# TensorE reads the addresses of a one-hot adjacency build four slots at a time

## The chip, the core and the metric

One core of a Trainium2 chip runs one program. The metric is the device time of one execution in microseconds (us), lower is better. Times of single instructions are in nanoseconds (ns) where marked.

## What is computed

A graph with 3125 nodes, 256 features and 100,000 edges sorted by destination goes through a normalised two-layer graph network with edge weights and then through a two-layer graph attention network, each with a residual connection.

```python
h = jnp.maximum(_layernorm(x, axis=-1), 0.0)
# L0: twice, for (W1, b1, g1, be1) and (W2, b2, g2, be2)
agg = jax.ops.segment_sum(w[:, None] * x[src], dst, num_segments=n)
x = gelu(layer_norm((x + agg) @ W + b, g, be))
# then x @ Wp + bp, residual, layernorm, relu
# L1: twice (8 heads, then 1)
e = leaky_relu(el[src] + er[dst])
alpha = exp(e - segment_max(e)[dst]) / denom[dst]
out = segment_sum(alpha[:, :, None] * feat[src], dst)
```

The part that matters here is the segment sum of the first network. The kernel does not gather rows for it. It first builds two dense tables in DRAM, the weighted adjacency (at_d) and the one of edge counts (mt_d), and then multiplies the features by the first.

## The kernel before

**The build.** The destinations are cut into windows of 4 nodes (WIN), two windows make a pair (392 pairs), 8 pairs one stage buffer (49 of them). The edges are cut into 1568 slots (S): a slot is up to 128 edges, one per partition, that belong to one window. For a slot the stationary operand is a one-hot of the low 7 bits of each edge's source (128 x 128, bf16), and the moving operand is a one-hot over 25 source blocks x 4 nodes of the window (100 columns), once plain and three times multiplied by the three bf16 parts of the edge weight. Three matmuls with 200, 100 and 100 columns (L1411, L1413, L1414) add the slot to its window in PSUM. Which window that is depends on the data, so the matmul's PSUM address comes from a register.

**Who does what.** VectorE (L555 to L565) makes the one-hots of 16 slots (SB, one batch, 98 batches) in three instructions: L560 the stationary one, L561 the moving one, L565 the products with the weight parts. They go to a ring of 3 batches (RB); L559 waits until TensorE has finished the slots of the batch three earlier (slot_done). TensorE waits for a batch's L565 ("weighted"). ScalarE drains a pair when its last slot is done (L1245, L1246 copies PSUM to the stage buffer, L1248 clears the bank and counts window_free up). It reads its own slot limits from at_end, four words every four pairs (L1239). PSUM has 8 banks, one per pair, so a slot may start only when the pair eight earlier has been drained: TensorE waits for window_free against a limit that also comes from a register. SyncE stores a full stage buffer as two transfers of 800 KB (L1833 to at_d, L1834 to mt_d), and after the last one starts to load the tables in pieces for the first convolution (L1845).

**The table.** VectorE computes for every slot its PSUM address and its limit, TensorE transposes both into bank 4, and two copies (L506, L507) lay them out in at_tab, for each batch 16 addresses and then 4 limits (that of every fourth slot). TensorE loads these 20 words into registers at the head of each batch (L1404), then waits for the batch, and per slot does the address arithmetic in one sequencer instruction and issues three matmuls. Instructions of an engine go out in order. The instructions that load registers, wait, or compute addresses are done by the engine's sequencer, which runs ahead of the array by what the queue holds.

**Around it.** Before the loop, eight matmuls (L1395) clear the banks. After it, the first convolution (L1444) begins when its first pieces have landed.

Of the kernel before, what the change touches and what calls it, by code (L numbers as in the profile page):

```python
# [6 lines left out]
I32 = mybir.dt.int32  # L7
# [6 lines left out]
P = 128  # L14
# [28 lines left out]
SB = 16  # L43
NSL = 13
# [4 lines left out]
NPAIR = 392  # L49
# [3 lines left out]
W2 = 2 * WC  # L53
# [101 lines left out]
def program(nc, x, src, dst, ew, w1, b1, g1, be1, w2, b2, g2, be2, wp, bp,  # L155
            gw1, al1, ar1, gw2, al2, ar2, out):
    ctx = ExitStack()
    with ctx:
        def sb(name, shape, dt=F32):
            return ctx.enter_context(nc.sbuf_tensor(name, shape, dt))  # L160

        def sem(name):
            return ctx.enter_context(nc.semaphore(name))
# [28 lines left out]
        br = sb("br", [4, P], I32)  # L192
        cr = sb("cr", [4, P], I32)

        at_tab = sb("at_tab", [NSL, P // SB, SB + SB // 4], I32)
        at_end = sb("at_end", [4, P], I32)
        wts = sb("wts", [P, 4384])
        w1s, w2s, wps = (wts[:, 512 * i:512 * (i + 1)].rearrange("p (k n) -> p k n", k=2) for i in range(3))
# [46 lines left out]
        def bank(i):  # L245
            return ps[:, 512 * i:512 * (i + 1)]
# [136 lines left out]
        slot_done, window_out, window_free = (sem(n) for n in ("slot_done", "window_out", "window_free"))  # L383
# [11 lines left out]
        V = Steps(sem("vector_step"))  # L395
# [22 lines left out]
        def vector(e):  # L418
            regs = [e.alloc_register(f"vb{i}") for i in range(4)]
# [53 lines left out]
            cs, vs, m4v, pf = (small[:, 128 + 16 * i:128 + 16 * i + NSL] for i in range(4))  # L473
# [29 lines left out]
            e.wait_ge(*V.last())  # L503
            e.scalar_tensor_tensor(out=vs, in0=vs, scalar=float(W2), in1=bkf, op0=ALU.mult, op1=ALU.add).then_inc(*V.inc("slot numbers"))
            e.wait_ge(pe_prep, PREP["regs"])
            e.tensor_copy(at_tab[:, :, 0:SB], bank(4)[0:NSL, 0:P].rearrange("p (b s) -> p b s", s=SB)).then_inc(*V.inc())  # L506
            e.tensor_copy(at_tab[:, :, SB:], bank(4)[0:NSL, P + 3:2 * P:4].rearrange("p (b s) -> p b s", s=SB // 4)).then_inc(*V.inc())  # L507
            e.tensor_copy(at_end[:, :], bank(4)[0:4, 2 * P:3 * P]).then_inc(*V.inc("regs"))


# [19 lines left out]
            for n in range(0, 12, 2):  # L530
                kk, i = divmod(n, 3)
                w = min(512, S - 512 * kk)
# [22 lines left out]
            for b in range(S // SB):  # L555
                r = b % RB
# [6 lines left out]
                w = t_parts[:, s0 // SG:(s0 + SB) // SG].rearrange("p g k (o s) -> p g k o s", o=1)  # L563
# [563 lines left out]
            for s in range(NS):  # L1127
                r = s % NR
                e.wait_ge(gh_in[r], 32 * (s // NR + 1))
                if s % 4 == 0:  # L1130
                    n = min(4, NS - s)
# [222 lines left out]
        def tensor(e):  # L1354
# [11 lines left out]
            vs, pf = small[:, 144:144 + NSL], small[:, 176:176 + NSL]  # L1366
# [4 lines left out]
            for n in range(12):  # L1371
                kk, i = divmod(n, 3)
# [13 lines left out]
                for k in range(4 * kk, min(4 * kk + 4, NSL)):  # L1386
                    f = (s_lo[:, P * k:P * (k + 1)], s_code[:, P * k:P * (k + 1)], srowf[:, k, 2 * P:3 * P])[i]
# [5 lines left out]
            e.wait_ge(act_table, 6)  # L1393
            for i in range(8):
                e.matmul(bank(i), ones[0:1, :], zrow, start=True, stop=True).then_inc(window_free, 1)  # L1395
            regs = []
            for s in range(S):
                b, i = divmod(s, SB)
                if i == 0:
                    k = s // P  # L1400
                    for r in regs:
                        e.free_register(r)
                    regs = [e.alloc_register(f"pb{b}_{n}") for n in range(SB + SB // 4)]
                    e.load(regs, at_tab[k:k + 1, s % P // SB, :])  # L1404
                    e.wait_ge(*V("weighted", b))
                if i % 4 == 0:
                    e.wait_ge(window_free, e.snap(regs[SB + i // 4], donate=True, min_val=1, max_val=NPAIR + 8))
                c = e.snap(regs[i], donate=True, min_val=0, max_val=7 * 512 + W2)
                g, z = divmod(i, SG)
                lo = ohr[:, b % RB, g, :, z]  # L1410
                e.matmul(ps[:, bass.ds(c, W2)].rearrange("p (k d) -> p k d", k=2), lo, mvr[:, b % RB, g, 2:4, :, z], start=False, stop=True,  # L1411
                         skip_group_check=True)
                e.matmul(ps[:, bass.ds(c, WC)], lo, mvr[:, b % RB, g, 0, :, z], start=False, stop=True, skip_group_check=True)  # L1413
                e.matmul(ps[:, bass.ds(c, WC)], lo, mvr[:, b % RB, g, 1, :, z], start=False, stop=True,  # L1414
                         skip_group_check=True).then_inc(slot_done, 1)
# [234 lines left out]
            for s in range(NS):  # L1650
                r, so = s % NR, s % 4
                b, before = RING["slot", s]
# [355 lines left out]

        block = ctx.enter_context(nc.Block())
        block.vector(vector)  # L2010
        block.scalar(scalar)
        block.tensor(tensor)
        block.gpsimd(gpsimd)
        block.sync(sync)
# [25 lines left out]
```

## Time and profile before

| | us |
|---|---|
| median of 3 runs | 3085.93 |
| lowest, highest | 3084.87, 3090.36 |
| the profiled execution | 3084.36 |
| its span, first to last instruction | 3082.6 |
| TensorE busy | 2588.9 (84%) |
| VectorE busy | 2350.3 (76%) |
| ScalarE busy | 1274.2 (41%) |
| GpSimd busy | 1000.1 (32%) |

Busy times are over the whole span and are an average over stages with different limits. The build stage is the first sixth of the span, up to 567 us. A q behind an engine's name marks an instruction of its sequencer. PE is TensorE's matmul, PEld its weight load, DVE is VectorE, ACT is ScalarE, POOL is GpSimd, SP is SyncE. An idle time is put down to the releaser whose event came last by the records.

### The profile page before, as it was taken

Reading aid. Unit: us, or ns where it says so; the run is one execution under the profiler, and the core shown is the slowest. Engines: PE = TensorE matmul, PEld = TensorE weight load, DVE = VectorE, ACT = ScalarE, POOL = GpSimd, SP = SyncE. Lnnn points to the kernel's source line nnn. Section 1 sums busy time; section 2 is a strip of 40 time slices with the busy share of each in tenths; the row PEclk is TensorE's granted clock in tenths of the full one; section 3 lists DMA queues with packets and bytes.
Section 4 is the critical chain, followed back from the end, with each engine's and each line's share of the span. In section 5 each row is a group of like instructions: output and inputs, shape, how many; then the busy total and the mean of one; then the engine's idle time right before and its main releaser. Section 6 shows DMA issues by size and latency. Waiting matters only on the chain.

```text
span 3082.6 us, 51075 instructions
## 1 busy us (share of the span) xinstructions
PE 2588.9 (84%) x18059; PEld 1968.9 (64%) x18059; DVE 2350.3 (76%) x3097; ACT 1274.2 (41%) x3089; POOL 1000.1 (32%) x1235
## 2 busy tenths in 40 slices
PE   5677767799989999989599999787777777757999
PEld 3666666454545555479588888565555556646888
DVE  7999999689633444488899999987777777666886
ACT  7777777202000111200255555465555554204443
POOL 3000000011110222303177777677777772011000
PEclk8888888899999999999799999899999999758999
DMA  4434344633447777334288888688877882432553
GB/s 142 167 155 172 159 163 162 239 113 120 127 138 251 254 265 258 119 105 126 73 233 228 233 226 229 167 233 217 217 217 217 217 217 92 139 88 70 167 164 103
DMA packets 311100, 538.18 MB, mean 175 GB/s; under 512 B 108482, under 2 KB 213460, under 8 KB 310596
## 3 DMA queue, kind: packets, MB, share of 16 engines
q1 hardware_dynamic: 241700, 309.63, 30.6%
q0 software_dynamic: 69152, 225.28, 25.7%
q8 instruction: 151, 2.47, 0.3%
q14 instruction: 97, 0.79, 0.1%
HBM read 420.89 MB, written 115.11 MB: 174 GB/s over the span
## 4 chain that ended last, share of the span: by engine, by line
PE 66%; DVE 21%; issue 5%; ACT 4%; DMA 2%; POOL 1%; DVEq 0%; POOLq 0%; SPq 0%; ACTq 0%
PE ps L1658 25%; PE ps L1444 15%; PE ps L1646 9%; DVE a L565 5%; PE ps L1579 5%; DVE a L560 3%; PE ps L1411 3%; PE ps L1357 2%; DVE a L561 2%; PE ps L1577 2%; DVE a L801 1%; PE ps L1413 1%; PE ps L1414 1%; PE ps L1470 1%; DVE a L833 1%
## 5 line engine op out<-in xcount | busy, mean ns | idle before, releaser
L1767 POOL DMA_INDIRECT a<-t,mid x502 | 483.2, 963 | 282.0 <-issue 143.6
L1444 PE MATMUL ps<-a 128*128 128x512 f32 x1200 | 557.4, 604 | 13.2 <-DVE a L742 13.2
L1658 PE MATMUL ps<-a,oh 128*128 128x260 f32 x2008 | 488.1, 390 | 79.0 <-issue 43.1
L1326 ACT ACTIVATE oht<-iota,mid 128x128 f32<-128x128 f32 x830 | 333.3, 402 | 441.0 <-PE ps L1658 399.1
L1658 PEld LDWEIGHTS ps<-a,oh 128*128 128x128 f32 x2008 | 366.5, 191 | 181.0 <-issue 85.1
L1411 PE MATMUL ps<-a 128*128 128x200 bf16 x1568 | 346.0, 277 | 143.5 <-DVE a L560 67.1
L1658 PE MATMUL ps<-wts,oh 128*128 128x260 f32 x1312 | 321.0, 393 | 59.3 <-ACT oh L1328 30.7
L1444 PEld LDWEIGHTS ps<-a 128*128 128x128 f32 x1200 | 219.3, 192 | 221.8 <-issue 215.3
L1137 DVE TENSOR_TENSOR a<-a,ps 128x1040 f32<-128x1040 f32 x251 | 309.6, 1234 | 55.6 <-DMA a<-t,mid 53.1
L1767 POOL DMA_INDIRECT wts<-t,mid x328 | 311.1, 949 | 111.0 <-issue 94.7
L1717 POOL TENSOR_SCALAR rstd<-mv 128x1 f32<-128x1 f32 x75 | 30.2, 403 | 955.7 <-DVE mv L452 953.5
L1413 PE MATMUL ps<-a 128*128 128x100 bf16 x1568 | 324.6, 224 | 0.0
L1414 PE MATMUL ps<-a 128*128 128x100 bf16 x1568 | 322.8, 224 | 0.0
L1658 PEld LDWEIGHTS ps<-wts,oh 128*128 128x128 f32 x1312 | 241.9, 192 | 125.7 <-ACT oh L1328 47.3
L1125 DVE TENSOR_TENSOR a<-a,ps 128x520 f32 x415 | 286.4, 690 | 7.4 <-PE ps L1658 3.0
L1646 PE MATMUL ps<-a,wts 128*128 128x257 f32 (+1 forms) x1250 | 271.5, 380 | 1.7 <-DVE wts L1083 1.7
L1411 PEld LDWEIGHTS ps<-a 128*128 128x128 bf16 x1568 | 168.3, 107 | 158.0 <-issue 157.9
L1328 ACT ACTIVATE oh<-oht 128x128 f32<-128x128 f32 x830 | 257.0, 310 | 26.2
L565 DVE TENSOR_TENSOR a<-a,mid 128x4800 bf16<-128x4800 bf16 x98 | 260.5, 2658 | 3.4
L1646 PEld LDWEIGHTS ps<-a,wts 128*128 128x128 f32 (+1 forms) x1250 | 234.4, 188 | 38.6 <-issue 1.8
L1246 ACT ACTIVATE a<-ps 128x400 f32<-128x400 f32 x392 | 193.1, 493 | 113.7 <-PE ps L1414 112.2
L1137 DVE TENSOR_TENSOR wts<-wts,ps 128x1040 f32<-128x1040 f32 x164 | 202.4, 1234 | 40.2 <-DMA wts<-t,mid 38.6
(325 smaller groups left out, 3946.8 us busy)
## 6 DMA issues: line engine op xcount, KB each, us to landing
a<-at_d SPq DMA_DIRECT2D x60, 1280.0 KB, 6.2
at_d<-a SPq DMA_DIRECT2D x49, 800.0 KB, 3.4
mt_d<-a SPq DMA_DIRECT2D x49, 800.0 KB, 5.6
a<-mt_d SPq DMA_DIRECT2D x30, 1280.0 KB, 6.1
a<-trlo_d SPq DMA_DIRECT2D x49, 512.0 KB
ot_d<-a SPq DMA_DIRECT2D x49, 320.0 KB, 6.0
a<-ot_d SPq DMA_DIRECT2D x49, 256.0 KB, 3.0
a<-t,mid POOLq DMA_INDIRECT x502, 3.8
```

The lines of the kernel that those rows point to most:

```text
L565: e.tensor_tensor(mvr[:, r, :, 0:3], bc(mvr[:, r, :, 3:4], five), bc(w, five), ALU.mult).then_inc(*V.inc(("weighted", b)))
L1125: e.tensor_tensor(d, d, pbig[RING["slot", s][0]].rearrange("p (u w) -> p u w", u=2)[:, :, 0:260], ALU.add).then_inc(head_add, 1)
L1137: e.tensor_tensor(bv, bv, col(exps_ps[:, s % 8, :], 65), ALU.mult).then_inc(head_mul, 1)
L1326: e.activation(oht[:, k, :], iota[:, :], ACT.Abs, bias=ndl[:, k, s:s + 1]).then_inc(*own.inc())
L1328: e.activation(oh[:, so, k, :], oht[:, k, :], ACT.Relu, bias=1.0, scale=-1.0).then_inc(head_oh, 1)
L1411: e.matmul(ps[:, bass.ds(c, W2)].rearrange("p (k d) -> p k d", k=2), lo, mvr[:, b % RB, g, 2:4, :, z], start=False, stop=True, skip_group_ ...
L1413: e.matmul(ps[:, bass.ds(c, WC)], lo, mvr[:, b % RB, g, 0, :, z], start=False, stop=True, skip_group_check=True)
L1414: e.matmul(ps[:, bass.ds(c, WC)], lo, mvr[:, b % RB, g, 1, :, z], start=False, stop=True, skip_group_check=True).then_inc(slot_done, 1)
L1444: m = e.matmul(acc[f].rearrange("p (x d) -> p x d", x=8), X[:, hi, P * f:P * (f + 1)], a, start=(hi == 0), stop=end, skip_group_check=True)
L1646: m = e.matmul(bank(u + j)[0:p, 0:D + 1], coef[t % R2][:, P * j:P * j + p], feat2[:, hi, :], start=(hi == 0), stop=(hi == NB - 1))
L1658: t = e.matmul(pbig[b][:, 512 * u:512 * u + 260], oh[:, so, k, :], hrows[2 * r + k][:, 260 * u:260 * (u + 1)], start=(k == 0), stop=(k == 1))
L1767: e.indirect_dma_start(out=hrows[2 * r + k], out_offset=None, in_=t2, in_offset=bass.IndirectOffsetOnAxis(ap=srci[:, k, s:s + 1], axis=0)) ...
```

## The change

at_tab becomes a plain row of 128 addresses for each 128 slots, and a new table at_free holds the limit of every eighth slot (16 for each 128 slots). TensorE loads four addresses ahead of every four slots (392 loads of 4 words), and four limits ahead of every 32 slots (49 loads of 4 words), in place of 20 words ahead of every 16 slots (98 loads). It waits for window_free once in eight slots, for the limit of the last of them, in place of once in four. The wait for the batch stays behind the loads of its first slots. VectorE still makes two copies for the tables.

```diff
--- before.py
+++ after.py
@@ -192,7 +192,8 @@
         br = sb("br", [4, P], I32)
         cr = sb("cr", [4, P], I32)
 
-        at_tab = sb("at_tab", [NSL, P // SB, SB + SB // 4], I32)
+        at_tab = sb("at_tab", [NSL, P], I32)
+        at_free = sb("at_free", [NSL, 16], I32)
         at_end = sb("at_end", [4, P], I32)
         wts = sb("wts", [P, 4384])
         w1s, w2s, wps = (wts[:, 512 * i:512 * (i + 1)].rearrange("p (k n) -> p k n", k=2) for i in range(3))
@@ -503,8 +504,8 @@
             e.wait_ge(*V.last())
             e.scalar_tensor_tensor(out=vs, in0=vs, scalar=float(W2), in1=bkf, op0=ALU.mult, op1=ALU.add).then_inc(*V.inc("slot numbers"))
             e.wait_ge(pe_prep, PREP["regs"])
-            e.tensor_copy(at_tab[:, :, 0:SB], bank(4)[0:NSL, 0:P].rearrange("p (b s) -> p b s", s=SB)).then_inc(*V.inc())
-            e.tensor_copy(at_tab[:, :, SB:], bank(4)[0:NSL, P + 3:2 * P:4].rearrange("p (b s) -> p b s", s=SB // 4)).then_inc(*V.inc())
+            e.tensor_copy(at_tab[:, :], bank(4)[0:NSL, 0:P]).then_inc(*V.inc())
+            e.tensor_copy(at_free[:, :], bank(4)[0:NSL, P + 7:2 * P:8]).then_inc(*V.inc())
             e.tensor_copy(at_end[:, :], bank(4)[0:4, 2 * P:3 * P]).then_inc(*V.inc("regs"))
 
 
@@ -1393,19 +1394,26 @@
             e.wait_ge(act_table, 6)
             for i in range(8):
                 e.matmul(bank(i), ones[0:1, :], zrow, start=True, stop=True).then_inc(window_free, 1)
-            regs = []
+            breg, freg = [], []
             for s in range(S):
                 b, i = divmod(s, SB)
+                k, w = divmod(s, P)
+                if s % 32 == 0:
+                    for r in freg:
+                        e.free_register(r)
+                    freg = [e.alloc_register(f"pf{s}_{n}") for n in range(4)]
+                    e.load(freg, at_free[k:k + 1, w // 8:w // 8 + 4])
+                if s % 4 == 0:
+                    for r in breg:
+                        e.free_register(r)
+                    breg = [e.alloc_register(f"pb{s}_{n}") for n in range(4)]
+                    e.load(breg, at_tab[k:k + 1, w:w + 4])
                 if i == 0:
-                    k = s // P
-                    for r in regs:
-                        e.free_register(r)
-                    regs = [e.alloc_register(f"pb{b}_{n}") for n in range(SB + SB // 4)]
-                    e.load(regs, at_tab[k:k + 1, s % P // SB, :])
                     e.wait_ge(*V("weighted", b))
-                if i % 4 == 0:
-                    e.wait_ge(window_free, e.snap(regs[SB + i // 4], donate=True, min_val=1, max_val=NPAIR + 8))
-                c = e.snap(regs[i], donate=True, min_val=0, max_val=7 * 512 + W2)
+                if i % 8 == 0:
+
+                    e.wait_ge(window_free, e.snap(freg[s // 8 % 4], donate=True, min_val=1, max_val=NPAIR + 8))
+                c = e.snap(breg[s % 4], donate=True, min_val=0, max_val=7 * 512 + W2)
                 g, z = divmod(i, SG)
                 lo = ohr[:, b % RB, g, :, z]
                 e.matmul(ps[:, bass.ds(c, W2)].rearrange("p (k d) -> p k d", k=2), lo, mvr[:, b % RB, g, 2:4, :, z], start=False, stop=True,
```

## Rows read from the trace of the kernel before

**Rows 1.** The page, TensorE's granted clock, 40 slices of 77 us.
```profile
PEclk8888888899999999999799999899999999758999
```

**Rows 2.** Groups by line, 60 to 570 us: shape, count, busy us, mean ns, idle before.
```profile
L1248 ACT ACTIVATE ps<-mzero 128x400 f32<-128x400 f32 x392 | 198.8, 507 | 12.4
...
L1246 ACT ACTIVATE a<-ps 128x400 f32<-128x400 f32 x392 | 193.1, 493 | 113.7 <-PE ps L1414 112.2
...
L560 DVE TENSOR_TENSOR a<-oh,a 128x2048 bf16<-128x2048 bf16 x98 | 119.6, 1221 | 29.0 <-PE ps L1414 29.0
```

**Rows 3.** The chain of waits, 60 to 580 us: start us, us, what.
```profile
84.17 1.14 DVE a L560
...
88.90 1.14 DVE a L560
...
553.12 2.67 DVE a L565
```

**Rows 4.** Single lines L560, L565, L1404: count, ns min/median/max, first to last start.
```profile
L560 DVE TENSOR_TENSOR a<-oh,a x98: 1217/1220/1227, 60.4 to 551.0; 128x2048 bf16<-128x2048 bf16 x98
...
L565 DVE TENSOR_TENSOR a<-a,mid x48: 2657/2657/2660, 62.6 to 298.5; 128x4800 bf16<-128x4800 bf16 x48
...
L1404 PEldq TENSOR_LOAD <-at_tab x48: 1357/1464/4112, 55.1 to 302.7; - x48
...
L1404 PEldq TENSOR_LOAD <-at_tab x1: 1364/1364/1364, 299.2 to 299.2; - x1
...
L1404 PEldq TENSOR_LOAD <-at_tab x1: 3626/3626/3626, 302.7 to 302.7; - x1
```

**Rows 5.** Stretches: us, busy (x count) PE PEld DVE ACT POOL, PEclk, DMA, GB/s.
```profile
300.00:301.00 1.00, 0.48 (x8) 0.33 (x7) 1.00 (x1) 0.97 (x4) 0.00 (x0) 1.00 0.00 0
...
302.00:307.00 5.00, 2.34 (x39) 2.20 (x37) 4.96 (x5) 3.65 (x8) 0.00 (x0) 1.00 0.81 328
```

**Rows 6.** Timeline of VectorE and TensorE around one load: start us, us, what, idle.
```profile
298.48 2.66 DVE L565 TENSOR_TENSOR a<-a,mid 128x4800 bf16<-128x4800 bf16 x1
...
303.45 0.25 PE L1411 MATMUL ps<-a 128*128 128x200 bf16 x1
...
303.63 0.25 PE L1411 MATMUL ps<-a 128*128 128x200 bf16 x1
...
303.76 0.21 PE L1414 MATMUL ps<-a 128*128 128x100 bf16 x1
...
306.63 0.26 PE L1411 MATMUL ps<-a 128*128 128x200 bf16 x1 [2.66 <-DVE a L565]
```

**Rows 7.** Line L1411, the sequencer's address arithmetic, once a slot; then one batch.
```profile
L1411 PEldq FUSED_REGOPS  x1568: 37/37/42, 65.3 to 565.1; - x196
...
L1411 PEldq FUSED_REGOPS  x16: 37/37/37, 306.5 to 308.5; - x16
```

**Rows 8.** Stretches around a long load.
```profile
309.60:310.20 0.60, 0.15 (x4) 0.02 (x2) 0.60 (x1) 0.57 (x2) 0.00 (x0) 1.00 0.00 0
...
313.10:316.00 2.90, 0.18 (x4) 0.03 (x1) 2.90 (x2) 1.99 (x5) 0.00 (x0) 0.99 0.87 353
...
316.00:319.30 3.30, 3.27 (x30) 3.06 (x31) 3.27 (x3) 1.70 (x4) 0.00 (x0) 0.50 0.00 0
...
320.90:324.00 3.10, 3.02 (x48) 2.96 (x48) 3.06 (x3) 3.00 (x7) 0.00 (x0) 1.00 0.65 255
```

**Rows 9.** Loads of four words on ScalarE (all, one under stores) and SyncE.
```profile
L1239 ACTq TENSOR_LOAD <-at_end x98: 305/406/907, 61.2 to 560.7; - x98
...
L1239 ACTq TENSOR_LOAD <-at_end x1: 747/747/747, 314.7 to 314.7; - x1
...
L1964 SPq TENSOR_LOAD <-cr x104: 293/298/500, 1517.1 to 2546.0; - x104
```

**Rows 10.** Timeline at the stage's end.
```profile
567.18 0.32 SPq L1833 DMA_DIRECT2D at_d<-a  x1
...
577.53 0.90 DVE L742 TENSOR_TENSOR a<-a,ident 128x128 f32<-128x128 f32 x4 [21.75 <-DMA a<-at_d]
```

## The prediction

> **What bounds the kernel now.** The change touches one loop, so I first placed it in time. The slices of the page [rows 1] are 77 us each and show TensorE's granted clock at 0.8 in the first eight and at 0.9 in most of the others; the table by line [rows 2] says what runs there: 1568 slots of three matmuls, between 62 and 567 us, VectorE building one-hots for 98 batches of 16 slots, and ScalarE draining 392 window pairs. Engine by engine: at full clock TensorE starts a slot (three matmuls) every 0.184 us (303.45 to 303.63, [rows 6]), 2.95 us a batch; ScalarE needs 0.49 + 0.51 us, 1.0 us a pair [rows 2], 4.0 us a batch of four pairs; VectorE, in the chain of waits [rows 3], goes round in 84.17 to 88.90 = 4.73 us when nothing holds it. Its L560 starts 98 times from 60.4 to 551.0 us [rows 4], which is 490.6 / 97 = 5.06 us a batch. So VectorE itself is held for 0.33 x 97 = 32 us, and L560 is the operation that waits for slots to be free (29.0 us idle behind TensorE, [rows 2]).
>
> TensorE, which has the shortest arithmetic, is therefore the engine that is late. The view of L1404 tells why [rows 4]: the register load of 20 words takes 1357 ns at best; of the 48 up to 302.7 us half take more than 1464 ns, up to 4112. The pair at 299.2 and 302.7 us took 1364 and 3626 ns. The windows over the same stretch [rows 5] show the difference: the DMA engines' share is 0.00 in 300 to 301 and 0.81 of 302 to 307, 4.0 us in all. These are the two 800 KB stores of a finished stage buffer, one pair of them for each 8 window pairs, two batches. The profile names VectorE as what ended the 2.66 us of idle at 306.63 [rows 6], but the batch that was wanted had been finished by the L565 that ran from 298.48 to 301.14 [rows 6]. By count: up to then there are 48 loads and 48 L565 [rows 4], one of each a batch, and the 48th L565 is that one. The named releaser had long been done. What ended last is the load, 302.7 + 3.63 = 306.4.
>
> How much of a load TensorE hides: it still started matmuls until 303.76, 1.0 us after the load began at 302.7. That is the queue the sequencer had filled ahead. A quiet load leaves about 0.6 us of nearly empty array (309.6 to 310.2, [rows 8]), a load under the stores 2.8 us.
>
> Sequencer time per two batches today: 16 slots issue in 306.5 to 308.5, so 0.12 to 0.13 us a slot against the array's 0.184 [rows 7]; 32 x 0.12 = 3.9, plus 1.36 + 3.63 of loads, plus about 0.2 around each, gives 9.3 us. Seen are 2 x (565.1 - 65.3) / 97.9 = 10.2 us [rows 7]. The missing 0.9 us is the clock: after 2.9 us of near idleness the next 3.3 us are granted 0.50 and hold 30 matmuls, where 3.1 us at 1.00 hold 48 [rows 8]. **Both costs hang on the one long load**, not on the matmuls.
>
> **The change part by part.** *Fewer words.* 98 loads of 20 words (1960 words) become 392 of 4 (L1404's successor) and 49 of 4 for the limits, 1764 words. What a load of 4 costs on TensorE is not in the trace. Below: 4/20 of 1357 ns, 0.27 us. Nearest rows, two other engines loading 4 words: 293 ns at best on SyncE and 305 at best on ScalarE; above: ScalarE's under the stores, 747 ns [rows 9]. I take 0.305 quiet and 0.75 under the stores, ScalarE's, because it loads in the same stretch. A load also has a seam: today the first slot of a batch comes 0.16 us after its load, which includes the batch's wait; I give 0.10 to each load and 0.1 more to each batch.
>
> *Where the loads fall.* Sequencer per two batches: 3.9 (slots) + 9 x 0.405 = 3.65 (eight address loads and one of limits) + 0.2 = 7.75 us without traffic. The stores are active about 4.0 us of it [rows 5]. Four slots in quiet take 0.49 + 0.405 = 0.90 us, under the stores 0.49 + 0.85 = 1.34 us, so 4.0 us of traffic lose 4.0 x (1 - 0.90 / 1.34) = 1.3 us. Sum 9.1 us for two batches, 4.55 a batch, against VectorE's 4.73. Were the load under the stores 1.0 us, the loss is 4.0 x (1 - 0.90 / 1.59) = 1.7 and the sum 9.5, level with VectorE's 2 x 4.73: the term is mild, since the traffic lasts 4.0 us whatever the loads do. It is also why splitting helps: before, the sequencer sat in one load while only 1.0 us of work was queued, and issued nothing; now it issues four slots between any two.
>
> *The clock.* No idle time of the array would pass about 0.6 us, the kind that the granted 1.00 survives today (309.6 to 310.2 between two stretches at 1.00, [rows 8]). So the 0.9 us per two batches goes too.
>
> *The limits.* One wait per eight slots for the eighth's pair instead of four waits a batch. The wait sits at the sequencer, with all later slots queued behind it, and ScalarE's drain must have come further by up to four slots, about one pair, of the 8 that the ring of banks allows. ScalarE needs 4.0 us a batch, plus at most 0.45 for its own load under the stores, against 4.73: it is not the bound. Taken at nothing; if ScalarE were 7 pairs late it would cost one pair, 1.0 us, per meeting.
>
> *The copies* to at_tab and at_free stay two, of 13 partitions and at most 128 words, and TensorE's first slot waits for much more than them. Nothing.
>
> **The sum.** VectorE becomes the bound. Its last L565 starts at 60.4 + 2.2 + 97 x 4.73 = 521.4 and ends at 524.1 (now 555.8, [rows 3]). TensorE then has one batch left: 0.2 + 16 x 0.12 + 3 x 0.405 + 0.4 for the last matmuls = 3.7, and ScalarE's last pair about 1 us more: the store L1833 would be issued at 529, now 567.18 [rows 10]. That is 38 us. All that follows (the first load of pieces, then the first convolution) hangs on it and moves as one; VectorE has been idle 21.75 us there [rows 10], and GpSimd has nothing in this stretch (0 instructions, [rows 5]). I take off 2 us for TensorE and VectorE being close to each other: 36. Profiled execution 3084.36 - 36 = 3048.4; the median of the runs is 1.6 above the profiled one: 3050.
>
> **The rivals.** *A: TensorE stays the bound, less so.* If loads average more than (9.46 - 4.1) / 9 - 0.10 = 0.50 us, VectorE is no longer the limit (my mean is (3.65 + 1.3) / 9 - 0.10 = 0.45, so this is near). At 9.7 us for two batches the stage ends at 68.9 + 49 x 9.7 + 3 = 547: 20 us gained, 3066. At 9.95, 3078. For it: 0.05 us of seam would do it.
>
> *B: slower.* A load on TensorE costs what it costs under the stores wherever it stands, 0.75 + 0.10, because the queue or VectorE's traffic rather than the stores slows it: 3.9 + 9 x 0.85 + 0.2 = 11.75 us for two batches, 1.55 more than now, 49 x 1.55 = 76 us: 3162. It decides from a mean load of (10.2 - 4.1) / 9 - 0.10 = 0.58 us on. Against it: the load at 299.2 ran at 1364 ns beside VectorE's L565 and a filled queue [rows 4, 6], 68 ns a word. The Trainium skill has a rule for this case, in Runtime: NRT & Kernel Launch, section "Instruction fetch mechanics": a register load costs about 200 ns a register, also in bulk. By it 4 words would be 0.8 us and the result near that of B. The trace has 68 ns a word in quiet and 180 under the stores, so the rule holds here for at most four tenths of the time.
>
> *C: the clock falls to its lower level and stays*, as the array's work is now spread thin: 30 matmuls in 3.3 us are 10 slots at 0.33 us [rows 8], and 16 of them are 5.35 us a batch, above VectorE's 4.73; 98 x 5.35 + 69 + 1 = 594, 27 us slower: 3113. Against it: at that level the array would be gapless, which is when it was granted 1.00 again at 319.3.
>
> *D: no change.* The gain is taken back, by ScalarE's limits (1.0 us for each of some 35 meetings) or behind the stage: 3080 to 3092.
>
> **How the numbers follow.** VectorE-bound, 3044 to 3054: 0.62. A, 3054 to 3078: 0.20. D: 0.07. B: 0.07. C: 0.04. A measurement of this kernel tells about 0.2%, 6 us, from no change. Faster 0.62 + 0.20 = 0.82, same 0.07, slower 0.11. Low end: VectorE's own pace allows no more than 38 us, and I add 5 for the stage's end and for what a median may differ by, 3043. High end: A's, 3078. B, C and D are left out, 0.18.
>
> **What would show it.** Right: L560 98 times from 60.4 to about 519 us with almost no idle; TensorE's idle in pieces under 1 us; the granted clock at or near 1.00 from 75 to 528; loads in clusters near 0.31 and 0.75. Wrong: a quiet load of 4 above 0.4 us; clock 0.50 in stretches; ScalarE as releaser of TensorE; the stage's end at 529 and the kernel not 36 us shorter.

## The result, and the profile after

The kernel after the change takes 3045.76 us (3044.32 to 3046.41, 4 runs) against 3085.72 us for the kernel before (3084.87 to 3090.36, 4 runs). The ratio is 0.9866, with a 95% interval of 0.9854 to 0.9879. That is 40 us less. The forecast was 3050 with 3043 to 3078 around it.

The profiled execution took 3046.41 us with a span of 3044.6. The whole gain of the span, 38.0 us, is in the build stage. The store L1833 of [rows 10] was issued at 567.18; the same store in the changed kernel is here, in the timeline at the end of the stage (start us, us, engine, line, operation):

```profile
528.73 0.49 ACT L1247 ACTIVATE a<-ps 128x400 f32<-128x400 f32 x1
529.25 0.32 SPq L1841 DMA_DIRECT2D at_d<-a  x1
```

567.18 - 529.25 = 37.9 us. What lies behind this point takes 2515.4 us before and 2515.3 us after (3082.6 - 567.2 and 3044.6 - 529.2).

The view of single lines of the changed kernel (count, ns min/median/max, first to last start) answers to [rows 4] and [rows 7]. L561 is VectorE's first instruction of a batch, L1405 the load of limits, L1410 the load of addresses, L1419 the address arithmetic, once a slot:

```profile
L561 DVE TENSOR_TENSOR a<-oh,a x98: 1215/1218/1222, 60.7 to 519.4; 128x2048 bf16<-128x2048 bf16 x98
...
L1405 PEldq TENSOR_LOAD <-at_free x49: 327/332/517, 55.3 to 518.4; - x49
L1410 PEldq TENSOR_LOAD <-at_tab x392: 327/334/1004, 55.9 to 527.0; - x196
...
L1419 PEldq FUSED_REGOPS  x1568: 37/37/42, 65.5 to 527.8; - x196
```

VectorE's round is (519.4 - 60.7) / 97 = 4.73 us, the undisturbed one of [rows 3]. The groups by line, 60 to 535 us, say the same from the other side: L561 waits for nobody (0.0, against 29.0 in [rows 2]), and ScalarE waits 67.4 us for TensorE in place of 112.2.

```profile
L561 DVE TENSOR_TENSOR a<-oh,a 128x2048 bf16<-128x2048 bf16 x98 | 119.3, 1218 | 0.0
...
L1247 ACT ACTIVATE a<-ps 128x400 f32<-128x400 f32 x392 | 194.3, 496 | 69.7 <-PE ps L1422 67.4
```

Two stretches of 50 us before and after (length, then busy and count of PE, PEld, DVE, ACT, POOL, then the granted clock, the DMA share, GB/s). Before:

```profile
120.00:170.00 50.00, 35.40 (x464) 33.26 (x463) 46.28 (x30) 37.24 (x79) 0.00 (x0) 0.86 0.41 165
```

After:

```profile
120.00:170.00 50.00, 38.41 (x523) 32.85 (x523) 49.65 (x32) 42.55 (x88) 0.00 (x0) 1.00 0.42 167
```

The granted clock is 1.00 where it was 0.86, and VectorE is busy for 49.65 of 50 us. From 75 us to the end of the stage the records of the granted clock have 33 stretches at 0.50 before, 119 us together, and one of 3.4 us after (at 285.3 us). In the table of waits (us in total, times, longest) the idle time of TensorE's weight loads on issue was in few and long pieces, and is in many and short ones. Before:

```profile
PEld ps L1411 <- issue: 157.9, 90, 3.4
```

After:

```profile
PEld ps L1419 <- issue: 146.7, 250, 1.5
```

The table of waits still names ScalarE as what ended 23.9 us of TensorE's idle time (39 times; 31.8 us before). In 31 of these 39 places (18.3 us) a load of TensorE ended later than the instruction that is named; in the other eight (5.6 us) ScalarE did end last. The matmul at 522.20 is one of the 31:

```profile
521.12 0.51 ACT L1249 ACTIVATE ps<-mzero 128x400 f32<-128x400 f32 x1
...
522.20 0.26 PE L1419 MATMUL ps<-a 128*128 128x200 bf16 x1 [0.73 <-ACT ps L1249]
```

```profile
L1410 PEldq TENSOR_LOAD <-at_tab x1: 950/950/950, 520.9 to 520.9; - x1
```

The clearing ended at 521.63. The load of the next four addresses ran from 520.94 to 521.89, under the stores, and ended last.

### The profile page after: what moved, and what is told of

It is laid out like the page before. It is cut to its first block, busy times and chain, and to the rows that moved or that the text cites. A ratio compares the mean times of both kernels' runs of the same rounds, so it can differ in the third digit from the quotient of the medians.

```text
span 3044.6 us, 51418 instructions
## 1 busy us (share of the span) xinstructions
PE 2586.2 (85%) x18059; PEld 1933.9 (64%) x18059; DVE 2346.9 (77%) x3097; ACT 1279.8 (42%) x3089; POOL 1000.1 (33%) x1235
## 4 chain that ended last, share of the span: by engine, by line
PE 62%; DVE 26%; issue 5%; ACT 4%; DMA 2%; POOL 1%; SPq 0%; DVEq 0%; POOLq 0%; ACTq 0%
PE ps L1666 26%; PE ps L1452 15%; PE ps L1654 9%; DVE a L566 8%; PE ps L1587 5%; DVE a L561 4%; DVE a L562 3%; PE ps L1358 2%; PE ps L1585 2%; DVE a L802 1%; PE ps L1478 1%; DVE a L834 1%; DVE a L601 1%; ACT oht L1327 1%; DVE a L1028 1%
## 5 line engine op out<-in xcount | busy, mean ns | idle before, releaser
L1419 PE MATMUL ps<-a 128*128 128x200 bf16 x1568 | 320.9, 256 | 108.7 <-issue 50.4
L1138 DVE TENSOR_TENSOR a<-a,ps 128x1040 f32<-128x1040 f32 x251 | 309.2, 1233 | 57.2 <-DMA a<-t,mid 54.9
L1421 PE MATMUL ps<-a 128*128 128x100 bf16 x1568 | 298.8, 208 | 0.0
L1422 PE MATMUL ps<-a 128*128 128x100 bf16 x1568 | 298.5, 208 | 0.0
L1419 PEld LDWEIGHTS ps<-a 128*128 128x128 bf16 x1568 | 152.9, 98 | 161.2 <-issue 146.7
L1138 DVE TENSOR_TENSOR wts<-wts,ps 128x1040 f32<-128x1040 f32 x164 | 202.2, 1233 | 36.1 <-DMA wts<-t,mid 34.7
L1247 ACT ACTIVATE a<-ps 128x400 f32<-128x400 f32 x392 | 194.3, 496 | 69.7 <-PE ps L1422 67.4
```

The source lines that it names most:

```text
L1138: e.tensor_tensor(bv, bv, col(exps_ps[:, s % 8, :], 65), ALU.mult).then_inc(head_mul, 1)
```

## The experiments

The stage is the place of everything here, so besides the whole time I give for each kernel the end of the stage and the pace of the slots, worked out from the first and the last start of the line with the address arithmetic: two batches take (last - first) / 97.9 x 2. That is 10.21 us before and 9.44 us after. The runs e5, e6, e7, e10 and e12 were made on chips on which all that lies behind the stage took some 180 us more, in the kernel before too (3273.87 us and 3271.61 us). The stage's pace is hardly touched by that: e12 has 10.21 us there, and e7, which by its ratio is level with the kernel before, has 10.28. The first slot comes up to 3 us later. All ratios are against the kernel before on the same chip. In the diffs `...` stands for code that is left out.

### e1: the split alone, with five words a load

```diff
-        at_tab = sb("at_tab", [NSL, P // SB, SB + SB // 4], I32)
+        at_tab = sb("at_tab", [NSL, P // 4, 5], I32)
...
-                if i == 0:
+                if i % 4 == 0:
...
-                    regs = [e.alloc_register(f"pb{b}_{n}") for n in range(SB + SB // 4)]
-                    e.load(regs, at_tab[k:k + 1, s % P // SB, :])
+                    regs = [e.alloc_register(f"pb{s}_{n}") for n in range(5)]
+                    e.load(regs, at_tab[k:k + 1, s % P // 4, :])
...
```

> One part alone: the loads are split (5 words ahead of every four slots: four addresses and their limit), the limits are waited for as before, once in four slots. Theory (the long load is what cost; the splitting is the change): a 5-word load is 0.37 to 0.40 us in quiet and about 1.1 under the stores, VectorE is the bound without idle, and the time is that of the changed kernel, 3046 to 3050 us, ratio 0.987 to 0.989. Rival 1 (the gain came from the rarer wait on window_free): no gain or little, 3080 us and more.

Measured: 3344.04 us, ratio 1.0834 (1.0816 to 1.0852). My expectation was wrong by some 295 us, and this miss taught the most. The time alone would fit rival 1, but the loads tell another cause. Twelve loads in order, in a stretch of 258 to 280 us, took 588, 1232, 1229, 1231, then 582, 3285, 1452, 1228, then 584, 1227, 1233, 1234 ns. **One load in four is fast.** The table's rows are 20 bytes apart, and every fourth row starts at a multiple of 16 bytes (counted from the start of the table, here and below). Of the 392 loads the 98 of that kind took 581 to 780 ns, all others at least 1227. The view of the line:

```profile
L1404 PEldq TENSOR_LOAD <-at_tab x392: 581/1235/3850, 55.1 to 823.9; - x196
```

### e2: the limits alone, with 18 words a load

```diff
-        at_tab = sb("at_tab", [NSL, P // SB, SB + SB // 4], I32)
+        at_tab = sb("at_tab", [NSL, P // SB, SB + SB // 8], I32)
...
-                if i % 4 == 0:
-                    e.wait_ge(window_free, e.snap(regs[SB + i // 4], ...))
+                if i % 8 == 0:
+                    e.wait_ge(window_free, e.snap(regs[SB + i // 8], ...))
```

> The other part alone: one load of 18 words ahead of every 16 slots (16 addresses, two limits), the limit waited for once in eight slots. Theory: TensorE's sequencer stays the bound, and each word less is 0.066 us in quiet and 0.18 us under the stores, so two batches save 2 x (0.066 + 0.18) = 0.5 us and the stage up to 24 us: 3062 to 3080 us, ratio 0.992 to 0.998, with loads in two clusters near 1.22 and 3.3 us and stretches at the lower clock still there. Rival 1 (the rarer wait is what gained): 3046 us.

Measured: 3253.61 us, ratio 1.0545 (1.0528 to 1.0563). Two words fewer, and 167 us more, where I had expected a gain: a second miss. Rows are 72 bytes apart now, so every second load starts 8 bytes off:

```profile
L1404 PEldq TENSOR_LOAD <-at_tab x98: 1584/3036/6778, 55.1 to 725.4; - x98
```

The 49 aligned loads took 1584 to 1781 ns, the others 4291 to 6778. Every second load is also the one that runs under the stores, as in the kernel before, so most of these long loads carry both costs. The first of them does not. It ran at 72.3 us, before the first stores:

```profile
L1404 PEldq TENSOR_LOAD <-at_tab x1: 4291/4291/4291, 72.3 to 72.3; - x1
```

```profile
71.60:76.40 4.80, 2.23 (x27) 2.00 (x24) 4.77 (x4) 2.84 (x6) 0.00 (x0) 0.86 0.01 3
```

So 4291 ns is the price of 18 words off a multiple of 16 bytes in quiet, known from this one load. These numbers and those of e1 fit one price list. A load that starts at a multiple of 16 bytes takes about 69 ns and 258 for each four words (4 words 327, 20 words 1357; 16 would be 1101), and a word left over costs almost as much as four: 581 - 327 = 254 for the fifth, (1584 - 1101) / 2 = 242 each for the seventeenth and eighteenth. A load that starts elsewhere pays for each word: (1227 - 69) / 5 = 232, (4291 - 69) / 18 = 235.

### e5: e1's loads with aligned rows

```diff
-        at_tab = sb("at_tab", [NSL, P // 4, 5], I32)
+        at_tab = sb("at_tab", [NSL, P // 4, 8], I32)
...
-                    e.load(regs, at_tab[k:k + 1, s % P // 4, :])
+                    e.load(regs, at_tab[k:k + 1, s % P // 4, 0:5])
```

> The same 392 loads of five words as in e1_split_only, but each row of the table is 8 words apart (32 bytes) in place of 5 (20 bytes), so every load starts at a multiple of 16 bytes. Theory (a load that starts at a multiple of 16 bytes reads four words at a time, some 256 ns each in quiet, and a word left over costs nearly as much; a load that starts elsewhere reads word by word at 231 ns): all loads are 581 to 590 ns in quiet, as the aligned fourth of e1's was; two batches take TensorE's sequencer 3.9 + 8 x 0.69 + 0.2 + 2.0 for the stores = 11.6 us, 3130 to 3170 us in all, against 3344 for e1. Rival (e1 was slow from five registers or from the number of loads, not from where they start): 3344 us again. The price of my forecast (0.07 us a word): 3050 us.

Measured: 3315.83 us, ratio 1.0133 (1.0113 to 1.0153), against 1.0834 for e1. The same five words in the same number of loads, only moved to multiples of 32 bytes:

```profile
L1404 PEldq TENSOR_LOAD <-at_tab x392: 576/590/1901, 57.6 to 614.3; - x196
...
L1412 PEldq FUSED_REGOPS  x1568: 37/37/42, 67.9 to 615.3; - x196
```

Two batches take 11.18 us where e1 took 15.53, and 11.6 was expected (the ratio makes some 3127 us on the first chip, just under the 3130 to 3170 forecast). So where a load starts accounts for 0.070 of e1's 0.083. The ratio is still over 1. e6 below has the same split with loads of four words and a load of limits for every 16 slots, and is at 0.9906, so the rest is the price of the fifth word.

### e7: the rarer wait alone

```diff
-                if i % 4 == 0:
-                    e.wait_ge(window_free, e.snap(regs[SB + i // 4], ...))
+                if i % 8 == 0:
+                    e.wait_ge(window_free, e.snap(regs[SB + i // 4 + 1], ...))
```

> The kernel before, loads of 20 words as they were, with only every second wait on window_free kept (for the limit of the eighth slot). Theory (the wait costs the sequencer nothing that shows): no change, 3083 to 3091 us. Rival 1 (the rarer wait gains by itself): 3070 us or less.

Measured: 3271.98 us, ratio 1.0001 (0.9991 to 1.0010). In the kernel before, the rarer wait by itself is worth nothing.

```profile
L1411 PEldq FUSED_REGOPS  x1568: 37/37/42, 65.8 to 568.9; - x196
```

### e6: the split with loads of four aligned words, limits as before

```diff
-                if s % 32 == 0:
+                if s % 16 == 0:
...
-                if i % 8 == 0:
...
+                if i % 4 == 0:
...
```

> The changed kernel with the limits as before: at_free holds every fourth slot's limit, four of them are loaded ahead of every 16 slots (98 loads in place of 49), and window_free is waited for once in four slots. So it is the split alone, with loads of four aligned words. Theory (the split is what gains; the limits give one load less per two batches): TensorE's sequencer needs 9.24 + 0.43 = 9.7 us for two batches against VectorE's 9.46, and the time is 3050 to 3062 us. Rival 1 (the rarer wait matters by itself): over 3070 us.

Measured: 3243.68 us, ratio 0.9906 (0.9887 to 0.9926), which on the first chip would be about 3057 us by my estimate. Two batches take 9.65 us, as worked out:

```profile
L1418 PEldq FUSED_REGOPS  x1568: 37/37/42, 68.5 to 540.8; - x196
```

From its first slot (68.5 us there, 65.5 in the changed kernel) the stage lasts 473.7 us against 463.7 after and 501.9 before. **So the split gives about 28 of the 38 us, and about 10 come from the change of the limits.** These are differences between chips: on the chip of e6 the stage of e7 lasts some 505 us, and by the intervals of the two ratios the limits may be worth anything from 2 to 22 us. That it is the saved load and not the rarer wait is argued from two numbers. The rarer wait was worth nothing in e7, and e6's 9.65 us is 0.41 more than TensorE's own pace with nine loads (9.24 in e4 below), which is one quiet load of 0.33 with its seam. That one load brings TensorE's sequencer from just below VectorE's 9.46 us to just above it. No run changes the wait alone in the split kernel.

### e3: the kernel before without the stores

```diff
...
-                e.dma_start(at_d[h, :, :], stage[:, h % 2, 0, :]).then_inc(at_out[h % 2], 16)
-                e.dma_start(mt_d[h, :, :], stage[:, h % 2, 1, :]).then_inc(at_out[h % 2], 16)
+                e.dma_start(at_d[h, :, 0:16], stage[:, h % 2, 0, 0:16]).then_inc(at_out[h % 2], 16)
+                e.dma_start(mt_d[h, :, 0:16], stage[:, h % 2, 1, 0:16]).then_inc(at_out[h % 2], 16)
...
```

> The kernel before with the suspected cause taken away: during the build each of the 98 stores moves only 16 elements a partition (8 KB in place of 800 KB); the tables are filled with 98 full stores from one buffer after the build (so they hold one buffer's contents, and some 200 us are added behind the stage). The stage alone is read. Theory (the stores stretch every second load): all 98 loads of 20 words at 1.36 us, granted clock near 1.00 from 75 us on, VectorE without idle, its last L560 at 519 us (551 before). Rival 2 (every second load is long by itself, from the parity of the batch or TensorE's queue): the long loads stay, last L560 near 551 us.

Measured, in a single run: 3236.94 us, with the added stores behind the stage in it. In the stage, with L561 and L1405 being the lines that answer to L560 and L1404:

```profile
L561 DVE TENSOR_TENSOR a<-oh,a x98: 1215/1218/1220, 60.5 to 519.3; 128x2048 bf16<-128x2048 bf16 x98
...
L1405 PEldq TENSOR_LOAD <-at_tab x98: 1356/1363/1559, 55.1 to 521.4; - x98
```

and, in the windows, the granted clock back at 1.00 with the DMA share at 0.03:

```profile
120.00:170.00 50.00, 32.12 (x498) 30.53 (x497) 49.65 (x32) 40.20 (x85) 0.00 (x0) 1.00 0.03 3
```

No load is long any more, and the last L561 starts at 519.3 as after the change. The stores are what stretches every second load of [rows 4], and taking them away gives the same stage as splitting the loads does (end 528.6 us, against 529.2). So loads of 20 words in quiet (98 of them) do not hold TensorE behind VectorE. The 2.3 us in excess of a quiet load, each two batches, and the lower clock behind it are what did.

### e4 and e12: VectorE's work cut, after and before the change

```diff
-                five = [P, SB // SG, 3, WC, SG]
-                e.tensor_tensor(mvr[:, r, :, 0:3], bc(mvr[:, r, :, 3:4], five), bc(w, five), ALU.mult).then_inc(*V.inc(("weighted", b)))
+                n = SB // SG if b < RB else SB // SG // 2
+                five = [P, n, 3, WC, SG]
+                e.tensor_tensor(mvr[:, r, 0:n, 0:3], bc(mvr[:, r, 0:n, 3:4], five), bc(w[:, 0:n], five), ALU.mult).then_inc(*V.inc(("weighted", b)))
```

> The changed kernel with VectorE's work cut: from the fourth batch on L565's products are made for the first half of the slots only (the other half keeps stale values), 1.3 us in place of 2.66, so VectorE could go at 3.4 us a batch. Theory (VectorE is the bound after the change, TensorE's sequencer next at 4.4 to 4.75 us a batch, ScalarE at 4.0): VectorE now waits for free slots, the stage shortens by 0 to 30 us, 3016 to 3046 us, most likely 3032. Rival 3 (TensorE is already the bound and VectorE's pace only happens to be the same): 3046 us, with VectorE idle for 1.3 us a batch. Rival 4 (ScalarE is next): the stage shortens by some 65 us, 2980 us.

> The kernel before with VectorE's work cut as in e4_short_vector (from the fourth batch on L565's products are made for the first half of the slots only; the other half keeps stale values). Theory (before the change TensorE's register loads are the bound, not VectorE, although the waits name VectorE): the stage ends at 560 to 567 us as before, 3078 to 3088 us in all, ratio 0.997 to 1.000. Rival (VectorE, named as releaser of TensorE for 106 us in the trace of before, was a bound too): the stage is 20 us or more shorter, ratio 0.993 or less.

Measured, e4 (on the changed kernel): 3035.05 us, ratio 0.9830 (0.9814 to 0.9847). The stage ends at 518.9, VectorE waits for free slots again, and the pace is TensorE's own:

```profile
L561 DVE TENSOR_TENSOR a<-oh,a 128x2048 bf16<-128x2048 bf16 x98 | 120.0, 1225 | 94.7 <-PE ps L1423 94.7
...
L1420 PEldq FUSED_REGOPS  x1568: 37/37/42, 65.4 to 517.5; - x196
```

(517.5 - 65.4) / 97.9 x 2 = 9.24 us for two batches, 4.62 a batch. Measured, e12 (the same cut on the kernel before): 3268.10 us, ratio 0.9995 (0.9986 to 1.0005). Two batches take 10.21 us, as in the kernel before:

```profile
L1412 PEldq FUSED_REGOPS  x1568: 37/37/42, 65.4 to 565.4; - x196
```

Before the change half of VectorE's largest instruction could be dropped for nothing. After it VectorE is the bound, by a small margin.

### e10 and e9: eight addresses a load

```diff
-                if s % 4 == 0:
+                if s % 8 == 0:
...
-                    breg = [e.alloc_register(f"pb{s}_{n}") for n in range(4)]
-                    e.load(breg, at_tab[k:k + 1, w:w + 4])
+                    breg = [e.alloc_register(f"pb{s}_{n}") for n in range(8)]
+                    e.load(breg, at_tab[k:k + 1, w:w + 8])
...
```

> The kernel of e4_short_vector (VectorE makes the products for half of the slots of a batch only, so TensorE's own pace shows) with eight addresses per load in place of four. Theory: a load of eight aligned words is 76 + 2 x 256 = 588 ns in quiet and about 1.8 us under the stores, half as many seams; two batches take 3.9 + 4 x 0.69 + 0.43 + 0.2 + 1.7 = 9.0 us against 9.24, 3020 to 3030 us. Rival (the fewer and longer the loads, the less the queue of 1 us covers, as in the kernel before): 3035 us or more.

> The changed kernel with eight addresses per load in place of four and nothing else. Theory (VectorE is the bound, so a faster TensorE gains nothing): the time of the changed kernel, stage end at 529 us, ratio to the kernel before 0.986 to 0.988, and more idle time of TensorE behind VectorE. Rival 3 (TensorE is still the bound after the change): the stage ends near 500 us, as in e10_eight_short.

Measured, e10: 3199.24 us, ratio 0.9772 (0.9746 to 0.9799), some 3015 us on the first chip, a little better than the 3020 to 3030 forecast; two batches take 8.76 us against e4's 9.24, by the first and last start of this row, and a load of eight words 585 ns at best:

```profile
L1411 PEldq TENSOR_LOAD <-at_tab x196: 585/601/2112, 58.8 to 495.8; - x196
...
L1420 PEldq FUSED_REGOPS  x1568: 37/37/42, 68.4 to 497.3; - x196
```

The loads that fall under the stores take up to 2.1 us here, twice the 1.0 us that the queue covers, and TensorE is faster all the same. Summed over the stage the loads, those of the limits among them, take 207 us in e10 and 217 in e4, and there are 196 fewer, each with a seam (59 ns in the median between a load's end and the next slot's arithmetic). How the 0.48 us divides between the two is not shown. Measured, e9 (the same on the changed kernel, VectorE untouched): 3044.29 us, ratio 0.9873 (0.9856 to 0.9889), stage end at 528.9. TensorE's faster sequencer gains nothing where VectorE is the bound. The interval overlaps that of the change, so e9 is not shown to be better.

### e8 and e11: a share of VectorE's products on GpSimd

```diff
...
+                n = SB // SG - PG
...
+                if i == SB - SG * PG:
+                    e.wait_ge(pool_part, PG * (b + 1))
...
+            for b in range(S // SB):
+                e.wait_ge(*V("codes", b))
+                for g in range(SB // SG - PG, SB // SG):
...
+                    e.tensor_tensor(mvr[:, b % RB, g, 0:3], bc(mvr[:, b % RB, g, 3:4], four), bc(w, four), ALU.mult).then_inc(pool_part, 1)
```

e8 has PG = 1 with four addresses a load, e11 has PG = 2 with eight.

> The changed kernel with one eighth of VectorE's products (L565: the last two slots of each batch, 600 of 4800 columns) made by GpSimd, which has nothing to do in this stage; TensorE waits for GpSimd's part ahead of slot 14. Theory (VectorE is the bound after the change at 4.73 us a batch): VectorE's round falls by 2.66 / 8 = 0.33 to 4.40 and TensorE's own pace, 4.62, becomes the bound, as in e4_short_vector: stage end near 520 us in place of 529, and some 9 us less in all than the changed kernel, ratio to the kernel before 0.983 to 0.985. Rival (GpSimd and VectorE get in each other's way in SBUF, or GpSimd needs over 4.7 us for its part): the three VectorE instructions get longer than 1.22, 0.98 and 2.33 us and the stage ends at 529 us or later.

> The same with two eighths of the products on GpSimd and eight addresses per load. Theory: VectorE's round 4.07 us, TensorE's sequencer 8.76 / 2 = 4.4 us a batch (from e10_eight_short), ScalarE 4.0 to 4.3: stage end at 500 to 505 us, 25 to 29 us less than the changed kernel, ratio to the kernel before 0.977 to 0.980. Rival (GpSimd's two parts take over 4.4 us a batch, or it slows VectorE): GpSimd becomes the releaser of TensorE and the stage ends at 529 us or later.

Measured, e8: 3109.91 us, ratio 1.0083 (1.0066 to 1.0100); e11: 3174.73 us, ratio 1.0294 (1.0277 to 1.0311). The rival was right, in its first form: the two engines get in each other's way. The timelines of VectorE and of GpSimd in e8:

```profile
300.92 2.35 DVE L569 TENSOR_TENSOR a<-a,mid 128x4200 bf16<-128x4200 bf16 x1
303.18 2.21 DVE L563 TENSOR_TENSOR a<-oh,a 128x2048 bf16<-128x2048 bf16 x1
305.31 0.98 DVE L564 TENSOR_TENSOR a<-oh,a 128x1600 bf16<-128x1600 bf16 x1
```

```profile
300.96 3.35 POOL L1752 TENSOR_TENSOR a<-a,mid 128x600 bf16<-128x600 bf16 x1 [2.06 <-DVE a L564]
```

Of VectorE's three instructions two keep their length (0.98, and 2.35 for seven eighths of 2.66), and L563, which follows while GpSimd still works, takes 2.21 us in place of 1.22. VectorE's round is 305.31 - 299.90 = 5.41 us. The Trainium skill says in SBUF — State Buffer, section "Terms", that VectorE and GpSimd share one pair of SBUF ports, which one of them holds for its full instruction while the other is blocked. The times agree with it. GpSimd's instruction lasts until 304.31, 1.05 us after L569 ended, and L563 lasts 1.08 us beyond that. So most of GpSimd's 3.35 us is waiting. e11 shows its work without VectorE beside it: the last of its 196 instructions of 600 columns runs when VectorE's last has ended, and takes 1180 ns, the least of the row:

```profile
L1752 POOL TENSOR_TENSOR a<-a,mid x196: 1180/2600/3039, 62.8 to 656.4; 128x600 bf16<-128x600 bf16 x196
```

## Why the prediction was right

**What bounds, and why.** Right. The named releasers of TensorE's idle time in [rows 6] were VectorE's instructions, the reading of the counts said they were innocent, and e12 and e3 show it: less VectorE work gains nothing, small stores gain it all in the stage (e3 is one run).

**The stage's end.** 529 was forecast and 529.25 measured. The 2 us taken off for TensorE and VectorE being close were not lost: L561 has 0.0 us of idle. That is half of the distance between 3050 and 3045.8. The other half is that I put the median 1.6 us above the profiled execution, and it came out 0.65 below it (3045.76 and 3046.41).

**The price of a load.** Of right size, and worked out wrongly. I set 0.305 us in quiet; it is 0.33. Under the stores I set 0.75, from ScalarE's row in [rows 9]; on TensorE two loads that ran wholly under them, at 303.3 and 304.9, took 912 and 947 ns, and 91 of the 392 loads lie between 900 and 1000 ns. The reason I gave, 68 ns a word, is wrong: the prices come in units of four words, 258 ns each. With four and twenty aligned words the two readings give nearly the same, which is why the forecast held. For any other count or start they do not, and e1 and e2 came out 257 and 167 us slower than the kernel before by it. Nothing in the trace of before could have shown it, since L1404's loads all had 20 words in rows of 80 bytes, and those of [rows 9] had four. That the change itself has loads of four words from multiples of 16 bytes was no part of my reasoning. In that the prediction was lucky: the same split with five words a load would have been forecast at the same time and lost 257 us. The price of 200 ns a register that stands beside rival B is not met by these loads (327 ns for four in quiet); it is near what a load off a multiple of 16 bytes costs for each word, 232 to 235 ns.

**TensorE's own pace.** 9.1 us for two batches forecast, 9.24 measured in e4. The mean load is (392 x 509 + 49 x 335) / 441 = 490 ns against the 0.50 at which I had VectorE cease to be the limit, so rival A was nearer than its chance of 0.20 said: with one load more for every nine, e6, TensorE is the bound (9.65 against 9.46).

**The traffic term.** I held that it is mild because the stores last 4.0 us whatever the loads do. With 0.93 in place of 0.75 the formula gives 1.6 in place of 1.3 us, and the sum 9.4; measured is 9.24. The seams were what I had too large: in e4's trace the next slot's arithmetic starts 59 ns (median) after a load's end, not 100. So a load too cheap and a seam too dear offset each other, and with the load alone put right the sum would have been level with VectorE's 9.46. This margin was luck in part.

**The clock.** Right: 1.00 in nearly the whole stage. How the loss divides between the load and the clock was taken from the sum alone (0.9 us of 10.2 in two batches for the clock). An estimate from the rows agrees: 119 us at the granted 0.50, in which 30 matmuls take 3.3 us where 48 take 3.1 at 1.00 [rows 8], lose 0.41 of their time, 49 us, or 1.0 us for two batches. No run takes away the one without the other, so this division is argued and not shown.

**The limits.** Right that the rarer wait is worth nothing, as far as e7 shows it, in the kernel before. Together with the load of limits that it saves it is worth about 10 us (e6); it stood in the sum as nine loads and not ten, and I had not told it as a gain of its own. ScalarE is still named as releaser of 23.9 us, which I had called a sign of being wrong; in 18.3 us of them a load ended last, and VectorE, which sets the pace, waits for neither.

**The rivals.** B (loads at the stores' price everywhere) fell by the row of L1410, median 334 ns. C (the clock stays low) by the windows. D by the stage's end at 529.25 and the 2515 us behind it, the same on both sides.

## What to carry to other kernels

Where the sequencer of an engine loads registers in line with its work, split a load that outlasts the work queued ahead of it by far (here 3.6 us against 1.0), and put the table so that each load starts at a multiple of 16 bytes and takes a multiple of four words. A split that breaks this second rule cost more than it gained (e1, e5). Four words a load are not the best size: eight, with twice the length under the stores, gave TensorE the shorter pace (e10). Look for such loads when an engine's idle time is put down to a releaser that, by count, had finished before: the profile does not count them as busy.

## What the runs showed of the hardware that I had not expected

The times of register loads on TensorE fit reads of four words at a time from a start at a multiple of 16 bytes: 4 words 327 ns, 8 words 585, 20 words 1357. A word left over costs 242 to 254 ns. From another start each word costs 232 to 235 ns, so that 5 words (1227 ns) take nearly as long as 20 aligned ones.

While two stores of 800 KB run, a load of four words takes about 0.9 us (912 and 947 ns) in place of 0.33; why is not shown. With the stores at 8 KB all 98 loads of the kernel before took 1356 to 1559 ns.

GpSimd's multiplication of 600 bf16 columns took 1.18 us alone and 3.35 us when it started just behind one of VectorE's, and stretched VectorE's next instruction from 1.22 to 2.21 us.
